# Four layers' modulation moved from a stage of its own into the first projection, with its products in column quarters of TensorE

## The reference, cut to what matters

```python
e = silu(c) @ emb_w + emb_b                 # layers 0 and 1: 1024 x 1024 weights
scale, shift = split(e, 2)
ada = silu(c) @ ada_w + ada_b               # layers 2 and 3: 1024 x 1536 weights
shift, scale, gate = split(ada, 3)
h = layer_norm(y) * (1 + scale) + shift     # where it is used
```

## Time and profile before

| | us |
|---|---|
| median of three runs | 6470.33 |
| the profiled execution, own time | 6471.62 |
| its span, first to last instruction | 6469.7 |
| TensorE busy | 5565.7 (86%) |
| VectorE busy | 4686.6 (72%) |
| ScalarE busy | 4209.5 (65%) |
| mean granted clock of TensorE | 0.962 |

### The profile page before, as it was taken

One profiled execution on the slowest core, in us unless ns is written; L12 is line 12 of the kernel. 1 busy time (PEld: TensorE's weight loads), 2 busy tenths in 40 slices (PEclk: granted clock), 3 DMA queues, 4 the chain that ended last, 5 costly groups with the idle time before them and its releaser, 6 DMA issues. The chain is left out here.

```text
span 6469.7 us, 86028 instructions
## 1 busy us (share of the span) xinstructions
PE 5565.7 (86%) x30592; PEld 3526.7 (55%) x30592; DVE 4686.6 (72%) x5716; ACT 4209.5 (65%) x6218; POOL 2483.9 (38%) x1098
## 2 busy tenths in 40 slices
PE   6999999998899989996688888887999578888884
PEld 2446666665355544443666666653444366666662
DVE  2328999996455445544999999974554699999993
ACT  1217888885222235554989898964555699999992
POOL 0000000000000000001999999970000499999994
PEclk8999999999999989997999999998999799999997
DMA  5335333332411033334556565633433655555654
GB/s 199 138 134 118 79 86 79 86 76 73 169 43 49 27 108 146 146 133 155 152 150 169 150 168 158 164 85 110 148 143 134 182 148 156 158 154 157 160 149 174
DMA packets 566989, 842.79 MB, mean 130 GB/s; under 512 B 102552, under 2 KB 241944, under 8 KB 566564
## 3 DMA queue, kind: packets, MB, share of 16 engines
q1 hardware_dynamic: 555108, 811.99, 42.9%
q0 software_dynamic: 5120, 16.78, 0.8%
q10 hardware_dynamic: 6336, 8.52, 0.4%
HBM read 544.27 MB, written 292.84 MB: 129 GB/s over the span
## 5 line engine op out<-in xcount | busy, mean ns | idle before, releaser
L1844 POOL TENSOR_TENSOR scan_hC<-scan_h,scan_Crep 128x1024 f32<-128x1024 f32 x1024 | 2395.6, 2367 | 2448.5 <-DVE scan_h L2077 2422.7
L2008 ACT ACTIVATE scan_a<-scan_dt,scan_A 128x512 f32<-128x512 f32 x2048 | 1367.9, 697 | 90.8 <-DVE scan_h L2077 73.3
L1878 PE MATMUL scan_y<-ident,scan_hC 128*128 128x128 f32 x8192 | 1111.6, 279 | 301.0 <-POOL scan_hC L1844 295.4
L1878 PEld LDWEIGHTS scan_y<-ident,scan_hC 128*128 128x128 f32 x8192 | 901.4, 141 | 691.0 <-POOL scan_hC L1844 643.1
L2077 DVE TENSOR_TENSOR_SCAN scan_h<-scan_a,scan_carry,scan_h 128x512 f32<-128x512 f32 x1024 | 1216.9, 1261 | 16.3 <-ACT scan_a L2008 13.1
L2077 DVE TENSOR_TENSOR_SCAN scan_h<-scan_a,scan_h 128x512 f32<-128x512 f32 x1024 | 1155.7, 1200 | 58.8 <-ACT scan_a L2008 58.4
L1984 ACT COPY scan_h<-scan_drive 128x1024 f32<-128x1024 f32 x1024 | 1042.0, 1018 | 166.1 <-PE scan_drive L1866 151.8
L1866 PE MATMUL scan_drive<-scan_Bd,scan_dT 128*128 128x256 f32 x4096 | 749.0, 305 | 126.5 <-ACT scan_h L1984 75.1
L1866 PEld LDWEIGHTS scan_drive<-scan_Bd,scan_dT 128*128 128x128 f32 x4096 | 557.4, 192 | 178.6 <-issue 94.6
L795 DVE CUSTOM_DVE_ANT_0 att_sm<-att_S,att_mneg 128x1024 f32<-128x1024 f32 x512 | 621.9, 1215 | 16.4 <-POOL att_mneg L721 16.1
L853 ACT ACTIVATE att_pr<-att_sm,att_nmax 128x1024 f32<-128x1024 f32 x512 | 590.7, 1154 | 57.8 <-DVE att_nmax L795 45.4
(11 more groups left out here) (189 smaller groups left out, 6256.2 us busy)
## 6 DMA issues: line engine op xcount, KB each, us to landing
scan_dT<-scratch_dtuT SPq DMA_DIRECT2D x512, 256.0 KB, 5.5
scratch_dtuT<-ssmin_dT SPq DMA_DIRECT2D x128, 512.0 KB, 3.5
scan_Crep<-scratch_bc SPq DMA_DIRECT2D x64, 1024.0 KB, 9.3
att_q<-scratch_q_split SPq DMA_DIRECT2D x256, 128.0 KB, 4.3
att_k<-scratch_k_split SPq DMA_DIRECT2D x256, 128.0 KB, 4.5
scratch_uD<-ssmin_uD SPq DMA_DIRECT2D x64, 512.0 KB, 3.4
scratch_z<-ssmin_zt SPq DMA_DIRECT2D x128, 256.0 KB, 2.1
scratch_dt<-ssmin_dt SPq DMA_DIRECT2D x64, 512.0 KB, 2.6
```

The lines of the kernel that those rows point to most:

```text
L1844: nc.gpsimd.tensor_tensor(hC[k % 2][:], of, Crep[:, 2 * p:2 * p + 2, :], ALU.mult).then_inc(s["scaled"].handle, 1)
L1878: last = nc.tensor.matmul(y[j][:, t, :], hC[k % 2][:, i, t * P:(t + 1) * P], ident[:], start=(p == 0 and i == 0 and t == 0), stop=False, i ...
L2008: nc.scalar.activation(a[(2 * k + i) % 3][:], dt[j][:], ACT.Exp, scale=A[:, m, 2 * p + i:2 * p + i + 1]).then_inc(s["decayed"].handle, 1)
```

## The change: what it does

The function `modulation` and its stage are gone. A class `Modulation` holds the same work in pieces, which `project` calls when it is given `scr`; only p0 is. p0 also takes its own scale and bias, the same for every batch, from the column tables, which it now loads itself in place of a table in scratch, and its mask from the input.

The products are done in three rounds. A round puts up to four blocks of 512 weight columns side by side: each is one product of a 128 x 32 stationary tile (the four batches, padded with zeros), and block q writes the partitions 32q to 32q + 31 of one PSUM bank. Rounds 0 and 1 have four blocks (both halves of two layers), round 2 has the two gates. That bank is taken from the ring of p0, which is left with seven.

```diff
+class Modulation:
+    def chunks(self, r):
+        if r < 2:
+            return [(2 * r + q // 2, q % 2) for q in range(4)]
+        return [(2, 2), (3, 2)]
+    def load(self, sp, r):
+        if r:
+            self.wait(sp, "rows", r)
+        for q, (l, chunk) in enumerate(self.chunks(r)):
+            src = self.io[("emb_w0", "emb_w1", "ada_w2", "ada_w3")[l]]
+            sp.dma_start(self.W[q][:], src[:, chunk * D:(chunk + 1) * D].rearrange("(k p) f -> p k f", p=P)
+                         ).then_inc(self.w_in[q].handle, 16)
+    def prepare(self, act):                 # silu, beside output 6 of batch 0
+    def make_A(self, act):                  # the two exponentials of A_log, beside output 10 of batch 0
+    def products(self, pe, r):
+        if r == 0:
+            self.wait(pe, "silu", 1)
+        else:
+            self.wait(pe, "read", r)
+        some = len(self.chunks(r))
+        for q in range(some):
+            pe.wait_ge(self.w_in[q].handle, self.w_in[q].at(16 * (r + 1)))
+        for k in range(ET):
+            for q in range(some):
+                last = self.nc.tensor.matmul(self.bank[32 * q:32 * q + 32, :], self.silu_c[:, k, :], self.W[q][:, k, :],
+                                             start=(k == 0), stop=(k == ET - 1))
+        last.then_inc(self.c["rows"].handle, 1)
+    def copy_rows(self, act, r):
+        self.wait(act, "rows", r + 1)
+        self.nc.scalar.copy(self.eb[:], self.bank[:]).then_inc(self.c["copied"].handle, 1)
+    def turn(self, pe, r):
+        self.wait(pe, "copied", r + 1)
+        for j in range(4):
+            last = self.nc.tensor.transpose(self.bank[:, j * P:(j + 1) * P], self.eb[:, j * P:(j + 1) * P], self.ident[:])
+        last.then_inc(self.c["turned"].handle, 1)
+    def plain_tables(self, dve):            # 9 small instructions
+    def tables(self, dve, r):               # waits for "turned"; 16 + 16 + 8 small instructions
+    def make_gates(self, dve):              # waits for "rows" 3; two additions of 4 x 512
+    def store(self, sp):                    # waits for "tables" 3; 5 tables, 2 gates, 1 mask, 2 of A
...
 def project(...)
+        beside = None if scr is None else Modulation(core, sb, psum, ident, io, scr, cols)
+        NB = 8 if beside is None else 7
+        banks = [psum(f"bank{k}", [P, HALF]) for k in range(NB)]
...     # TensorE, ahead of the entry
+                if beside is not None and it >= 1 and o == 2:
+                    beside.products(pe, it - 1)
+                if beside is not None and 1 <= it <= 2 and o == 8:
+                    beside.turn(pe, it - 1)
+                if e >= NB:
+                    before, of, which = entries[e - NB]
...     # ScalarE, behind the output
+                if beside is not None and it == 0 and o == 6:
+                    beside.prepare(act)
+                if beside is not None and it == 0 and o == 10:
+                    beside.make_A(act)
+                if beside is not None and 1 <= it <= 2 and o == 5:
+                    beside.copy_rows(act, it - 1)
...     # VectorE
+                if beside is not None and it == 0 and o == 10:
+                    beside.plain_tables(dve)
+                if beside is not None and 1 <= it <= 2 and o == 12:
+                    beside.tables(dve, it - 1)
+                if beside is not None and it == 3 and o == 6:
+                    beside.make_gates(dve)
...     # SyncE
             rows.load(sp, 1)
+            if beside is not None:
+                beside.load_consts(sp)
+                beside.load(sp, 0)
...     # behind the store of an output
+                    if beside is not None and 1 <= it <= 2 and o == 4:
+                        beside.load(sp, it)
+                    if beside is not None and it == 3 and o == 12:
+                        beside.store(sp)
...
-        modulation(core, ident, io, scr, cols)
```

More of the change, by code:

```diff
@@ L150, in _ @@
                                     base=0, pattern=[[-1, P]], channel_multiplier=1)
[L154 to L273, removed]
-                for k in range(KT):
-                    nc.vector.tensor_scalar(tab[:, t, :, k], e[:, l, scale0 + k], 1.0, col(w, k), ALU.add, ALU.mult)
-                    last = nc.vector.tensor_scalar(part[:, l, k], e[:, l, scale0 + k], 1.0, col(b, k), ALU.add, ALU.mult)
-                step(last)
-                for k in range(KT):
-                    last = nc.vector.tensor_tensor(tab[:, t, :, 4 + k], part[:, l, k], e[:, l, shift0 + k], ALU.add)
-            last.then_inc(dve_done.handle, 1)
-    core.consts_in.stage_added(80)
-    for k in range(3):
-        w_in[k].stage_added(32 if k == 0 else 16)
-    w_free[0].stage_added(1)
-    core.vector_step.stage_added(4)
-    core.scalar_step.stage_added(1)
@@ L342, in load_table @@
     def load_table(self, sp):
+        if self.plain is not None:
+            cols, src = self.plain[0], self.plain[3]
+            sp.dma_start(cols[:], src).then_inc(self.tab_in.handle, 16)
+            return
         sp.dma_start(self.tab[:], self.tab_src.rearrange("b p e -> p b e")).then_inc(self.tab_in.handle, 16)
@@ L395, in take @@
         h, kt = o // KT, o % KT
+        if self.plain is not None:
+            w_at, b_at = self.plain[1] + kt, self.plain[2] + kt
+            scale, bias = self.plain[0][:, w_at:w_at + 1], self.plain[0][:, b_at:b_at + 1]
+        else:
+            scale, bias = self.tab[:, it, kt:kt + 1], self.tab[:, it, 4 + kt:5 + kt]
         if it == 0 and o == 0:
@@ L425, in project @@
         sb, psum = allocator(nc, ctx, name)
-        rows = Rows(core, sb, 2, src, tab, func, eps, ident)
+        plain = (cols, COL_AT["norm_w0"], COL_AT["norm_b0"], io["cols"]) if tab is None else None
+        rows = Rows(core, sb, 2, src, tab, func, eps, ident, plain=plain)
         xT = rows.xT
@@ L443, in value_of @@
             return part_of(slot, 0) if split else stage[slot][:]
-        banks = [psum(f"bank{k}", [P, HALF]) for k in range(8)]
+        beside = None if scr is None else Modulation(core, sb, psum, ident, io, scr, cols)
+        NB = 8 if beside is None else 7
+        banks = [psum(f"bank{k}", [P, HALF]) for k in range(NB)]
         outs = []
@@ L480, in _ @@
             for e, (o, it, k) in enumerate(entries):
-                bank = e % 8
-                if e >= 8:
-                    before, of, which = entries[e - 8]
+                bank = e % NB
+                if beside is not None and it >= 1 and o == 2:
[4 more added lines that the diff above has]
+                    before, of, which = entries[e - NB]
                     if before is None:
@@ L508, in _ @@
             for e, (o, it, k) in enumerate(entries):
-                bank, uses_ = e % 8, e // 8 + 1
+                bank, uses_ = e % NB, e // NB + 1
                 if o is None:
@@ L527, in _ @@
             nonlocal steps
+            if beside is not None:
+                beside.clear(dve)
             for k in range(TT):
@@ L586, in _ @@
             if keep is not None:
-                sp.dma_start(kp[:], keep.rearrange("b p e -> p b e")).then_inc(core.consts_in.handle, 16)
+                sp.dma_start(kp[:], keep).then_inc(core.consts_in.handle, 16)
             rows.load(sp, 1)
+            if beside is not None:
+                beside.load_consts(sp)
+                beside.load(sp, 0)
             for it in range(B):
@@ L608, in _ @@
                     sp.dma_start(dst, tile).then_inc(stored[slot].handle, 16)
+                    if beside is not None and 1 <= it <= 2 and o == 4:
+                        beside.load(sp, it)
+                    if beside is not None and it == 3 and o == 12:
+                        beside.store(sp)
             for k in range(8):
                 sp.wait_ge(stored[k].handle, stored[k].at(16 * B * uses))
+            if beside is not None:
+                beside.stored(sp)
     rows.stage_added()
+    if beside is not None:
+        beside.stage_added()
     core.consts_in.stage_added(n_const)
@@ L616, in project @@
     for k in range(8):
-        full[k].stage_added(len(entries) // 8)
+        full[k].stage_added(sum(e % NB == k for e in range(len(entries))))
         staged[k].stage_added(B * uses)
@@ L976, in _ @@
             load_row(1, 3)
-            sp.dma_start(kp[:], scr["keep"][1].rearrange("b p e -> p b e")).then_inc(ci, 16)
+            sp.dma_start(kp[:], scr["keep"].rearrange("b p e -> p b e")).then_inc(ci, 16)
             load_weight(3, "film_out_W")
@@ L1680, in scan @@
         O = psum("O", [P, D])
-        s = {n: core.count("scan_" + n) for n in ("cleared", "driven", "laid", "decayed", "scanned", "carried", "scaled", "turned",
+        s = {n: core.count(n) for n in ("cleared", "driven", "laid", "decayed", "scanned", "carried", "scaled", "turned",
                                                   "y_full", "gated", "A_in")}
@@ L2177, in program @@
     scr = {}
```

(7 more changed lines are left out.)

101 lines of the change are left out of this document (98 added, 3 removed).

## The result

The changed kernel took 6384.7 us (median of four runs, 6369.16 to 6392.2) against 6469.39 us before, in the same session. The ratio is 0.9866, 95% interval [0.9847, 0.9885], a gain of 84.7 us where 83 were forecast; 6387 us was predicted.

What follows compares the result with a forecast made beforehand. TensorE bounds p0 without idle time, and the modulation's stage ahead of it costs its whole length. 6471.62 - 105.35 + 21.0 + 0.9 = 6388.2 us profiled, less 1.29 for the median: 6387 us, range 6378 to 6400 us.

Steps and rivals of the forecast that it cites:

- What is removed: Modulation's stage ahead of p0: 105.35 us go, p0 starts that much earlier, 2 us either way for TensorE's warming.
- The products: Three rounds on TensorE within p0: 48 groups of 0.429 us plus three times 0.14 us, 21.0 us added.
- (a): Rival on the rounds: overlap less complete, a factor of 1.17 on every group, 24.0 us, time 6390 us; chance 0.09.
- The turns: Two turns of four transposes in TensorE's list, 0.43 us each, add 0.9 us together.
- The borders: TensorE's array going over to quarters and back: 0.14 us a round, 0.4 us for three, within the products' 21.0.
- Waits at nothing: TensorE's waits in p0 for ScalarE's copy, VectorE's reading and the weights add nothing, all being done outputs ahead.
- The seventh bank at nothing: p0's ring without its eighth bank costs nothing: seven cover six outputs, 20.6 us, above VectorE's worst lag of 11 us.
- The queue of SyncE at nothing: Stores behind weight loads of 21.7 us don't stop TensorE; a load would have to take over 45 us, 186 GB/s.
- (c): Rival on SyncE's queue: stores late behind weights stop TensorE in batches 1 and 2; 6401 us at 160 GB/s; chance 0.04.
- (b): Rival on the rounds: no overlap, blocks go one by one, 68.6 us, time 6434 us; chance 0.05.
- (d): Rival on p0's clock: TensorE stays at half clock after a round, 247 us more, time 6634 us; chance 0.02.
- The sum: Whole program: 6471.62 - 105.35 + 21.0 + 0.9 = 6388.2 us profiled, 6387 us as median, a gain of 83 us.

Runs made afterwards that it cites:

- the serial run: Changed kernel with the two product loops exchanged, each block's eight contraction steps in a row, one block behind the other: 0.9927 of the kernel before.
- one step of eight: Changed kernel with only one contraction step of eight in each round, so the tables hold wrong values: 6369.75 us, 0.985 of the kernel before.
- two banks: Changed kernel with two PSUM banks instead of seven in the first projection's ring: 6437.58 us, 0.9936 of the kernel before.
- loads3: Changed kernel with each round's weights loaded three times, one load after the other, holding up the stores: 6445.36 us, 0.9954 of the kernel before.
- the second session: The changed kernel run again with no edit, beside the kernel before: 6396.05 us, 0.9882 of the kernel before.

## Why the prediction was right, step by step

- **What is removed**, 105.35 us: p0 begins at 4.33 us. Its first transposes come at 20.34 us, where 20.15 was worked out, and batch 0's second transposes 104.96 us earlier than before. Of the 0.39 us between, 0.19 stand ahead of the first transposes and the rest in the first outputs, where TensorE comes to full speed; that is within the 2 us allowed, and the serial run was 2.2 us faster there. The granted clock says nothing of it: it reads 1.00 from 20 to 30 us, while the outputs' weight loads come 0.85 us apart up to 28.5 us and 0.43 apart behind that. The old stage had one wait for weights, of 20.3 us, and not two.
- **The products**, 21.0 us: 7.00 + 7.00 + 6.99 us. 16 groups of 0.429 are 6.87 us, so the excess inside a round is 0.13 us, much as attention's 1.00 over 0.86. It does not grow with the columns, and (a) is refuted: a factor of 1.17 would have made each round 8.0 us. The serial order, 57.2 us for the three, shows what the overlap is worth: 36.2 us. The Trainium skill ("TensorE: Matmul & The Clock Gate", "Measured speedup vs the span model") has 2.38 times for three column tiles and 3.07 for four row tiles. The estimate of 9.0 us a round from it was too high: this case measures 27.47 / 7.00 = 3.9 times for four column tiles.
- **The turns**, 0.9 us: 0.44 each.
- **The borders**, 0.4 us: too low. The 0.14 us read from attention is only what lies inside a piece. Outside it, the 16 records ahead of round 0 take 125.67 - 118.70 = 6.97 us and the 48 behind it 153.37 - 132.67 = 20.70, each 0.10 us over their length at 0.429. With these a round costs 0.34 us beyond its groups, 1.0 us for the three, and so 22.47 us came back on TensorE where 21.9 were counted.
- **Waits at nothing**: right. No wait for VectorE, ScalarE or a DMA stands in TensorE's list between batch 0's start and p0's end. That the rounds are not hidden behind anything either, one step of eight showed.
- **The seventh bank at nothing**: right, and two banks show where the cover ends. The reasoning was loose in one point. I counted a bank ring as six outputs, 20.6 us, everywhere. Between outputs 8 and 15 half of its entries are transposes, and there it covers 14 us. VectorE's lag at the tables was put too high: the output behind them is done at 179.34 us, 1.8 us late, and the next one is on time.
- **The queue of SyncE at nothing**: right for one load, wrong in its threshold. A load had to take 45 us to stop TensorE, I said, a rate of 186 GB/s. By the 42.6 us of loads3, and 2.8 for the store, 39.8 us are enough, an estimate of 211 GB/s. In rival (c) the price of a slow load was too low by the same cause. A small slip beside it: the 380 GB/s of the deep queue is 389 when a KB is 1024 bytes, as in the 8.39 MB.
- **(b) and (d)**: the granted clock from 60 to 380 us is 1.00, and the blocks overlap. (b) also had too high a price, since even in the serial order three rounds take 57.2 and not 68.6 us.
- **The sum**: 83.4 us worked out, 82.5 us in the trace, 84.7 us in the times. The last agrees so well partly by luck, since medians of four differ by some 10 us: the second session gave 72 us. Both medians lie in the range of 6378 to 6400 us.
- **The sign of being wrong**: I had written that the stages behind p0 should keep their lengths within a few us. In the two profiled executions they differ by 20 us, so by that sign the forecast was wrong, and only the second trace of the same kernel showed that the sign was bad: stages that nobody touched vary by more than it allowed.

## What to carry to other kernels

Here a stage that only prepares what is needed later cost its whole length, its loads and its stores included. Within a stage that one engine bounds without slack it costs that engine's instructions and nothing else, so the work is to make these few: 80 thin products went into 24 steps of up to four, interleaved step by step, and 20 steps do as well. What covers a queue that is held up is counted in the ring's entries at that place, not in the largest of them.

## What the runs showed of the hardware

- Four products in column quarters, 128 x 32 by 512 columns, take as long as two do: 7.00 us for 64 records and 6.99 us for 32. The length goes by groups, 0.43 us each.
- Blocks queued one behind the other in different quarters overlap at their border only, by four records (5 us of 27.5).
- The array going over to quarters and back cost 0.34 us a round: 0.13 us inside, 0.10 in the outputs ahead and 0.10 to 0.11 in those behind.
- With waits of 2.3 and 11.6 us between rounds the granted clock fell (0.66 on the mean from 40 to 60 us), and rounds of 7.0 us took 8.8 to 9.9.
- The granted clock read 1.00 at the start of the program while records were spaced as at half speed, 0.85 us.
- Loads of blocks 512 columns wide ran at 386 to 387 GB/s, as did p0's own loads, also 512 wide, before the change (386). The old stage's, 1024 columns wide, ran at 416. The width as the cause is not tested.
